# An order of steps written out for each engine, three idle PSUM banks taken into use, and two projections as 64-token column tiles

## The reference, cut to what matters

```python
# layer 0: non-local attention (32 inner channels)
th, ph, g = conv1x1(x, Wt, bt), conv1x1(x, Wp, bp), conv1x1(x, Wg, bg)
a = softmax(einsum('bci,bcj->bij', th, ph), -1)
x = conv1x1(einsum('bij,bcj->bci', a, g), Wo, bo) + x
t = to_tokens(x)                      # (4, 256, 64)
# layer 1: causal attention, 4 heads of 16, then a mixture of 8 experts
t = t + attn(layernorm(t), W_attn, W_proj)
t = t + experts(layernorm(t))         # gate weights from a mean over the batches
x = from_tokens(t)
```

## Time and profile before

| | us |
|---|---|
| median of 3 runs (lowest, highest) | 77.64 (77.51, 77.99) |
| time of the profiled execution | 77.84 |
| its span, first to last instruction | 76.0 |
| outside the span | 1.84 |
| PE busy | 66.5 (87%) |
| DVE busy | 47.9 (63%) |
| ACT busy | 36.1 (47%) |
| POOL busy | 15.9 (21%) |

### The profile page before, as it was taken

One profiled execution on the slowest core, in us unless ns is written; L12 is line 12 of the kernel. 1 busy time (PEld: TensorE's weight loads), 2 busy tenths in 40 slices (PEclk: granted clock), 3 DMA queues, 4 the chain that ended last, 5 costly groups with the idle time before them and its releaser, 6 DMA issues.

```text
span 76.0 us, 1446 instructions
## 1 busy us (share of the span) xinstructions
PE 66.5 (87%) x535; PEld 43.6 (57%) x535; DVE 47.9 (63%) x145; ACT 36.1 (47%) x74; POOL 15.9 (21%) x27
## 2 busy tenths in 40 slices
PE   3999984958896989999999999799959999999960
PEld 1328963946774774676667765457246274556520
DVE  2020668988589799089759955980551964799460
ACT  0604543072375067407640954249754458697500
POOL 3000033333320591041033203260312300000000
PEclk9999999999999999999999999999999999999999
DMA  0895000000000000000000000000000000000003
GB/s 5 238 301 237 0 0 0 0 0 0 9 0 4 0 0 0 0 9 0 0 0 0 0 0 9 0 0 4 0 0 0 0 0 9 0 0 0 0 34 103
DMA packets 961, 1.83 MB, mean 24 GB/s; under 512 B 120, under 2 KB 569, under 8 KB 955
## 3 DMA queue, kind: packets, MB, share of 16 engines
q1 hardware_dynamic: 732, 1.54, 6.2%
q10 hardware_dynamic: 222, 0.21, 1.1%
HBM read 1.48 MB, written 0.26 MB: 23 GB/s over the span
## 4 chain that ended last, share of the span: by engine, by line
PE 64%; DVE 13%; issue 8%; ACT 8%; POOL 3%; POOLq 0%; ACTq 0%
PE A L667 27%; PE M L667 15%; PE Q L667 10%; PE PR L667 8%; ACT p L456 4%; DVE m L599 3%; DVE m L595 3%; PE Q L687 2%; DVE m L565 2%; DVE th_s L495 2%; DVE ph_s L495 2%; POOL diag L307 1%; ACT h L412 1%; POOL ln_rs L362 1%; POOL xsum L392 1%
## 5 line engine op out<-in xcount | busy, mean ns | idle before, releaser
L307 POOL TENSOR_TENSOR diag<-neg_ident,m 128x256 fp32r<-128x256 f32 (+1 forms) x8 | 6.6, 826 | 21.6 <-DVE m L565 13.4
L362 POOL TENSOR_TENSOR ln_rs<-ln_var,half 128x2 f32<-128x2 f32 x8 | 5.6, 700 | 21.0 <-DVE ln_var L538 21.0
L412 ACT ACTIVATE h<-PR,bn_c,bn_s 128x256 f32<-128x256 f32 (+1 forms) x13 | 7.8, 637 | 2.1 <-PE PR L667 2.0
L402 ACT ACTIVATE qk_tmp<-PR 128x512 fp32r<-128x512 f32 x8 | 4.3, 594 | 7.5 <-PE PR L667 7.5
L456 ACT ACTIVATE p<-A 128x512 f32<-128x512 f32 (+1 forms) x8 | 6.0, 808 | 2.9 <-PE A L667 2.9
L552 DVE TENSOR_SCALAR ln_xs<-t,ln_mv,ln_rs 128x128 f32<-128x128 f32 x16 | 4.8, 343 | 3.3 <-POOL ln_rs L362 3.3
L667 PE MATMUL M<-warm 128*128 128x512 bf16 x10 | 4.4, 629 | 1.2 <-DVE warm L497 1.2
L667 PE MATMUL M<-p,v 128*32 128x256 f32 (+1 forms) x64 | 4.9, 333 | 0.4 <-ACT p L456 0.2
L599 DVE TENSOR_REDUCE m<-A 128x4 f32<-128x1024 f32 x4 | 4.9, 1214 | 0.0
L595 DVE TENSOR_REDUCE m<-A 128x4 f32<-128x512 f32 x4 | 2.8, 691 | 3.0 <-PE A L667 2.8
L402 ACT ACTIVATE f_tmp<-Q 128x512 fp32r<-128x512 f32 x4 | 2.4, 598 | 4.7 <-PE Q L667 4.7
(11 more groups left out here) (134 smaller groups left out, 138.8 us busy)
## 6 DMA issues: line engine op xcount, KB each, us to landing
pack_ffn<-in_pack_ffn_dram SPq DMA_DIRECT2D x1, 712.0 KB, 5.9
pack_attn<-in_pack_attn_dram SPq DMA_DIRECT2D x1, 276.0 KB, 3.9
out_dram<-o_sb SPq DMA_DIRECT2D x2, 128.0 KB, 1.7
x<-in_x_dram SPq DMA_DIRECT2D x1, 195.0 KB
pack_conv<-in_pack_conv_dram ACTq DMA_DIRECT2D x1, 130.5 KB
pack_ident<-in_pack_ident_dram ACTq DMA_DIRECT2D x1, 70.0 KB, 3.6
x<-in_x_dram SPq DMA_DIRECT2D x1, 65.0 KB
```

Of the source, the lines that this page charges most:

```text
L307: return engine.tensor_tensor(out, neg_ident[:, :].unsqueeze(1).to_broadcast([P, n, P]), m.unsqueeze(2).to_broadcast([P, n, P]), ALU.mult)
L362: pool.tensor_tensor(ln[i]["rs"][b][:, :], ln[i]["var"][b][:, :], half[:, 0:NB], ALU.pow).then_inc(ln[i]["s_pow"], 1)
L402: return act.activation(out, in_, ACT.Copy)
L412: act.activation(out, bank, ACT.Relu, bias=bn_c[:, i, q:q + 1], scale=bn_s[:, i, q:q + 1]).then_inc(relu_ok[s], 1)
```

## The change

The front no longer comes from the slot table. Each of PE, ACT, DVE and POOL gets a tuple `front` of (step, batch) pairs, and the slot table takes over from slot 7 (`FRONT_SLOTS`), which begins with the attention scores of batch 0. Three banks that stood idle at the time are used: the transposed scores go to A[2] for even batches and Q[0] for odd ones, and the weighted values of batches 0 and 2 go to PR[1] and Q[1], those of batch 1 to M. One filler matmul goes. DVE's layer-norm statistics become a step of their own (3.05); those of batch 3 and the normalization of batches 2 and 3 now stand in slot 7. Steps 5 and 9 split each half of 128 tokens in two column tiles of 64, so that eight instructions take the place of four. The residuals of batches 2 and 3 are issued in turn. The waits are those that the new banks need. The diff, cut to its core (only the import of itertools and unchanged lines are left out):

```diff
@@
         sums = [A[:, 2, 0:N], M[:, N:2 * N]]
-        pv1 = [bank[:, 0:NB * (C + 1)].rearrange("p (n c) -> p n c", n=NB) for bank in (A[:, 1, :], A[:, 0, :], A[:, 1, :], M)]
+        pv1 = [bank[:, 0:NB * (C + 1)].rearrange("p (n c) -> p n c", n=NB) for bank in (PR[1], M, Q[1], M)]
+        s1t = [(A[:, 2, :], Q[0])[b % 2] for b in range(B)]
         vps = Q[0][:, 0:NB * C]
@@
-        FILL = {"loads": 10, 1: 1, 2: 1}
-        CONV_STEPS = 4
+        FILL = {"loads": 10, 1: 1}
+        BATCH_OF = {2.8: 3, 3: 3, 3.05: 3, 3.1: 2, 3.15: 3}
         KEYS_ON_PE = 1
...
                       12.0: (0, 1, 0), 12.1: (0, 1, 1), 12.2: (0, 1, 2), 12.3: (0, 1, 3), 13.0: (1, 0, 0)}
+        FRONT_SLOTS = 7
         SLOTS = 1 + ATTN_SLOT[10] + 2 * (B - 1)
...
                 return FFN_SLOT[step] if b == 0 else None
-            if step in (0.9, 1):
-                return b + 1 if (b < 2) == (step == 1) else None
-            if step in (3.1, 3.2) and (b == B - 1) != (step == 3.2):
-                return None
-            if step == 3.2:
-                return ATTN_SLOT[6.2]
+            if step in BATCH_OF:
+                return FRONT_SLOTS if b == BATCH_OF[step] else None
             if step in (10, 10.2) and (b == 2) != (step == 10.2):
...
                 return None
-            if step < CONV_STEPS:
-                return int(step) + b
             return ATTN_SLOT[step] + 2 * b
...
         def schedule(*order):
-            for slot in range(SLOTS):
+            for slot in range(FRONT_SLOTS, SLOTS):
                 for step in order:
@@
-            for step, b in schedule(9, 6, 10, 10.2, 7, 0.9, 1, 3):
-                if step in (0.9, 1):
+            front = ((1, 0), (1, 1), (1, 2), (3, 0), (1, 3), (3, 1), (3, 2))
+            for step, b in itertools.chain(front, schedule(9, 6, 10, 10.2, 7, 3)):
+                if step == 1:
                     if b == 0:
@@
-            for step, b in schedule(8, 10.2, 11.3, 0, 0.1, 2, 5.1, 5.2, 10, 8.2, 5, 11.0, 11.1, 5.6, 7, 11.2, 12.0, 12.2, 4):
+            front = ((0, 0), (0.1, 0), (0, 1), (0.1, 1), (0, 2), (0.1, 2), (2, 0), (0, 3), (0.1, 3), (2, 1), (2, 2), (4, 0),
+                     (2, 3), (5.1, 0), (5.2, 0), (4, 1), (5.6, 0), (5, 0))
+            for step, b in itertools.chain(front, schedule(8, 10.2, 11.3, 5.1, 5.2, 10, 8.2, 5, 11.0, 11.1, 7, 11.2, 12.0, 12.2, 4)):
                 if step == 0:
@@
                     act.wait_ge(s1t_ps, b + 1)
-                    act.activation(p1[b][:, :, :], Q[(b + 1) % 2][:, :].rearrange("p (n i) -> p n i", n=NB),
+                    act.activation(p1[b][:, :, :], s1t[b].rearrange("p (n i) -> p n i", n=NB),
                                    ACT.Exp).then_inc(p1_ok, 1)
@@
-            for step, b in schedule(6, 8.1, 6.1, 6.2, 3.2, 0.9, 1, 3, 0, 5.1, 5.3, 3.1, 9, 12.1, 9.1, 12.3, 8, 7, 2):
+            front = ((0, 0), (1, 0), (0, 1), (0, 2), (1, 1), (1, 2), (2, 0), (0, 3), (3, 0), (3.05, 0), (1, 3), (3.1, 0),
+                     (3, 1), (3.05, 1), (3, 2), (3.1, 1), (5.1, 0), (3, 3), (3.05, 2))
+            for step, b in itertools.chain(front, schedule(6, 8.1, 6.1, 6.2, 3.1, 5.1, 5.3, 3.05, 3.15, 9, 12.1, 9.1, 12.3, 8,
+                                                           7)):
                 if step == 0:
...
                                 Q[b % 2][:, i * N:(i + 1) * N]).then_inc(f_split, 1)
-                if step in (0.9, 1):
+                if step == 1:
                     v.wait_ge(s1_ps, b + 1)
@@
                     i.then_inc(t1_ok, 1)
+                if step == 3.05:
                     layer_norm(0, b, t1[b], t1_ok)
-                if step in (3.1, 3.2):
+                if step in (3.1, 3.15):
                     normed(0, b, t1[b])
@@
-            def residual(b):
-
-                pe.wait_ge(t2_ok, b + 1)
+            def residual(*batches):
+
+                pe.wait_ge(t2_ok, batches[-1] + 1)
                 for n in range(NB):
-                    side = (b % SB) * C
-                    mm(sums[b // SB][side:side + C, n * P:(n + 1) * P], t2[b][:, n, :], ident, start=(n == 0),
-                       stop=False)
+                    for b in batches:
+                        side = (b % SB) * C
+                        mm(sums[b // SB][side:side + C, n * P:(n + 1) * P], t2[b][:, n, :], ident, start=(n == 0),
+                           stop=False)
@@
-            for step, b in schedule(8, 10.2, 6, 8.1, 8.15, 0.9, 3, 0, 0.1, 1, 2, 2.1, 5.1, 5, 10, 8.2, 8.25, 11.0, 7, 7.1, 5.5, 9,
-                                    11.2, 12.0, 12.2, 9.9, 4):
+            front = ((0, 0), (0.1, 0), (0, 1), (0.1, 1), (1, 0), (0, 2), (0.1, 2), (2, 0), (1, 1), (2.1, 0), (1, 2), (0, 3),
+                     (0.1, 3), (2, 1), (3, 0), (1, 3), (2.1, 1), (2, 2), (2.1, 2), (3, 1), (2, 3), (3, 2), (4, 0), (2.1, 3),
+                     (5.1, 0), (3, 3), (5, 0), (4, 1), (5.5, 0))
+            for step, b in itertools.chain(front, schedule(8, 10.2, 6, 8.1, 8.15, 5.1, 5, 10, 8.2, 8.25, 11.0, 7, 7.1, 9, 11.2,
+                                                           12.0, 12.2, 9.9, 4)):
                 if step == 0:
@@
                         pe.wait_ge(f_split, 2 * (b - 1))
-                    if b > 2:
-                        pe.wait_ge(p1_ok, b - 2)
                     for i in range(2):
@@
                     last.then_inc(vx_ps, 1)
-                if step in (0.9, 1):
+                if step == 1:
...
                         pe.wait_ge(m1_ok, b - 1)
-                    if b > 2:
-                        pe.wait_ge(t1_ok, b - 2)
                     if b == 0:
@@
-                    pe.wait_ge(f_split, 2 * min(b + 2, B))
-                    if b == 0:
-                        keep_busy(2, Q[(b + 1) % 2][:, :])
+                    pe.wait_ge(f_split, 2 * (3 if b == 1 else b + 1))
                     if b > 1:
...
                     for n in range(NB):
-                        mm(Q[(b + 1) % 2][:, n * N:(n + 1) * N], ph_s[b][:, n * P:(n + 1) * P], th_s[b][:, :],
+                        mm(s1t[b][:, n * N:(n + 1) * N], ph_s[b][:, n * P:(n + 1) * P], th_s[b][:, :],
                            start=(n == 0), stop=False)
...
                     for n in range(NB):
-                        last = mm(Q[(b + 1) % 2][:, n * N:(n + 1) * N], ones_r[:, :],
+                        last = mm(s1t[b][:, n * N:(n + 1) * N], ones_r[:, :],
                                   diag1[b][:, :, :].rearrange("p n i -> p (n i)"), start=False, stop=(n == NB - 1))
...
-                    pe.wait_ge(m1_ok, min(b + 2, B))
+                    if b == 2:
+                        pe.wait_ge(f_split, 2 * B)
+                    if b == 3:
+                        pe.wait_ge(t1_ok, 2)
                     pe.wait_ge(p1_ok, b + 1)
@@
                     else:
-                        pe.wait_ge(p1_ok, B - 1)
+                        pe.wait_ge(t1_ok, B - 1)
                         pe.wait_ge(ln[0]["s_TT"], b)
...
-                    pe.wait_ge(p1_ok, B)
+                    if b == 0:
+                        pe.wait_ge(p1_ok, B)
+                    else:
+                        pe.wait_ge(v_ok, b)
                     if b > 2:
...
                     for n in range(NB):
-                        last = mm(vps[:, n * C:(n + 1) * C], xT[b][0:C, n * P:(n + 1) * P], attn_v)
+                        for t in range(2):
+                            last = mm(vps[t * C:(t + 1) * C, n * C:(n + 1) * C],
+                                      xT[b][0:C, n * P + t * C:n * P + (t + 1) * C], attn_v)
                     last.then_inc(v_ps, 1)
@@
                         pe.wait_ge(v_const, 5)
-                        pe.wait_ge(t1_ok, B - 1)
+                        pe.wait_ge(m1_ok, B)
+                        pe.wait_ge(p1_ok, B - 1)
                     pe.wait_ge(q_ok, b + 1)
@@
                     for n in range(NB):
-                        last = mm(Q[0][:, n * C:(n + 1) * C], yT[b][:, n * P:(n + 1) * P], attn_proj)
+                        for t in range(2):
+                            last = mm(Q[0][t * C:(t + 1) * C, n * C:(n + 1) * C],
+                                      yT[b][:, n * P + t * C:n * P + (t + 1) * C], attn_proj)
                     last.then_inc(pj_ps, 1)
@@
             pe.wait_ge(cw_ok, 1)
-            for b in range(SB, B):
-                residual(b)
+            residual(SB, SB + 1)
             second_layer(2, 2)
...
             third_layer(0, 3)
```

More of the change, by code:

```diff
@@ L1 @@
 from contextlib import ExitStack
+import itertools
 import numpy as np
```

## The result

The changed kernel takes 75.46 us (median of six executions), the one before 77.58 (also of six) in the same series. The ratio is 0.969, 95% interval 0.964 to 0.974, which is 2.4 us (2.0 to 2.8). Some executions of nearly every version, the one before too, are 1.5 to 12% longer; they are in these two medians but not in the ratios, and nothing is read from a stretch that such an execution lengthened.

A forecast was written before the change was run, and what follows sets the result against it. Bounds: engine hand-offs in the front up to 25.41 us, then attention turns as a loop, with PE nearly continuous behind. 77.84 - 1.5 (front) - 0.5 (tiles) = 75.8, median 0.20 lower: 75.6 us, range 74.7 to 76.6.

The forecast's parts named there:

- The front: Everything before the first attention maximum at 25.41 us; the new order brings it 1.5 us earlier, bounds 1.1 to 1.8.
- The walk: Front events timed in the new order from the old trace's durations and distances; queries' copy at 20.15 against 21.67.
- the bounds given for the hand-offs: In the front, hand-offs of 0.13 to 0.15 us shrink where PE loaded weights ahead, four times, +0.3.
- 0.4 to spare: Normalization of batch 0 on DVE ends at 17.7, 0.4 us before PE's transposes of batch 0 at 18.07.
- They hide under ACT's copies: Transposes of batch 1, at about 21.0 on PE, hide under ACT's copies of queries and keys.
- each 0.1 us goes straight onto the keys: If batch 1's transposes are late in the front, each 0.1 us of it delays the keys.
- The moved layer norm: Layer-norm work moved into DVE's first attention turn leaves 0.2 us spare; cost nothing, bound +0.6.
- Column tiles: 64-token tiles gain 0.24 us each in the projections of batches 2 and 3, 0.5 in all; bounds -1.1 and 0.6.
- The residuals in turn: Alternating residuals of batches 2 and 3, followed by a block waiting for an ACT ReLU: 0, bound 0.1 either way.
- The rule against these tiles: Same-row tiles' weight loads would not overlap matmuls; eight loads alone 0.43 us, gain mostly gone; the trace was held to disagree.
- The clock: Rival: without the filler, PE's granted clock falls in the front, three us lost, 78.6; chance 0.04.
- The sum: Whole kernel: 1.5 us from the front and 0.5 from column tiles, 77.84 to 75.8, median 75.6.

The follow-up runs named there:

- the norm-first order: The changed kernel with DVE doing batch 0's output and layer-norm statistics before splitting batch 3, PE and ACT reordered too; ratio 0.971 to the kernel before.
- The six copies: The changed kernel with six more unused 128 x 128 copies on DVE in the first attention turn; ratio 0.974 to the kernel before.
- the order-alone run: The changed kernel with the blocks of steps 5 and 9 back at 128 tokens, without column tiles; ratio 0.983 to the kernel before.

## Why the prediction was right

- **The front, 1.5 us forecast, 1.71 measured.** The walk named the right events in the right order, and they came at most 0.35 us earlier than walked. On the old axis (0.12 subtracted) scores of batch 2 came at 11.73 (forecast 11.72), theta and phi of batch 3 at 12.04 (12.12), batch 3's scores at 14.75 (14.94), the normalization's end at 17.71 (17.7), the copy of the queries at 19.96 (20.15). What was mis-sized is small: from theta and phi to their copy 1.06 in place of 1.17 where PE had its weights ahead, and from the exponential to the values 0.05 (15.62 + 0.60 to 16.27) in place of 0.13. Both were within the bounds given for the hand-offs.
- **"0.4 to spare" was wrong, without a price.** The normalization of batch 0 ended at 16.94 + 0.89 = 17.83, and with the hand-off of 0.13 the transposes could start at 17.96, which they did (17.97). That its end met the forecast's 17.7 is luck: on the old axis it began at 16.82, some 0.3 earlier than walked, and took 0.89 for the 0.60 of the sum (the last section has the reason). PE, 0.2 earlier than walked, was ready for the transposes at about the same time. DVE's chain and PE's were equally long here, so neither alone could have been shortened with profit; the norm-first order shortened both.
- **"They hide under ACT's copies" was wrong, by 0.14 us.** The transposes of batch 1 are copied ahead of the keys on ACT, and with 128-token values they come too late. The forecast had named the price ("each 0.1 us goes straight onto the keys") but set the overrun to nothing; the tiles of batch 0's values, which I had costed at nothing, took it away again. From the queries' copy to the maximum it was 23.82 - 20.08 = 3.74, as forecast, by these two errors together; without the tiles it was 3.88 (23.96 - 20.08, where the copy of the queries is at 20.08 as well).
- **The moved layer norm cost nothing,** as forecast: 0.29 us of DVE's idle time are left for the 0.2 of the sum, and the turn is 7.24. The six copies put the reserve at 0.37.
- **Column tiles, 0.5 us from two projections, measured 0.54, but as 0.20 and 0.34 and not as twice 0.24.** The tiled block of batch 2 takes 51.37 - 51.00 = 0.37 to its successor, not the 0.31 that I took from the weighted values' pace. For batch 3 I had only looked at the projection itself. From its start to the second expert block behind it were 59.65 - 58.19 = 1.46, now 57.44 - 56.38 = 1.06, so 0.40 are gone there (0.34 reach the end), more than the 0.24 of the sum and more than the 0.55 - 0.37 = 0.18 of a tiled block by itself; the timeline lists the first matmuls of the expert block between it and the projection's last ones. Why these two run into each other now was not tested. The sum was met in part by luck: one size too large, the other too small. The other six were worth nothing, but for the values of batch 0 above. The turns were not shortened by the tiled values or by the projections of batches 0 and 1. The residuals in turn, set to 0 with a bound of 0.1, gave 0.05, and with them the 0.60 behind the first maximum is complete (0.54 + 0.05 + 0.01 in the first turn).
- **The rule against these tiles** (the Trainium skill, "TensorE: Matmul & The Clock Gate", Part 3, "What overlaps and what doesn't": a weight load overlaps running matmuls only if the row group differs) does not hold here. Eight loads and eight matmuls of one row group took 0.37 us to the successor; by the estimate in the prediction from that page the loads alone would take 0.43.
- **The clock** did not fall in the front without the filler: in the changed kernel's page all slices are full. In the order-alone run it fell only in the last half microsecond of the span (0.64), about 2 us after PE's last matmul.
- **The sum** was 2.0 us for 2.31 in the trace (1.71 + 0.60) and 2.4 (2.0 to 2.8) in time. The mechanism was right in both parts; what it fell short by is the hand-offs in the front (0.2) and the crumbs behind it (0.1).

## What to carry to other kernels

A wait on a buffer and a place in an in-order queue hide each other: free banks alone gave 0.00 us, the new order on the old banks 0.61, both together 1.71. Judge such changes together, by a walk over one iteration with durations and start-to-start distances from the trace; it met the events named above within 0.2 us, the exponentials and values in between within 0.35. And a faster block is worth something only where the trace shows no other engine ending the next wait: of eight tiled blocks, five gave nothing, and the other three 0.14, 0.20 and 0.34.

## What was not expected of the hardware

- The first matmul on x starts between 5.18 and 5.97 us after the span's start in profiles of these kernels, with the same instructions ahead of it. That alone is 1% of the time, as much as the smaller effects here, and counting from this matmul brought repeated events to 0.01 us (17.87 and 17.86).
- DVE took longer beside POOL, which the walk had left out. In the new order the diagonal of batch 3 runs on POOL while DVE normalizes batch 0. The timeline of the changed kernel, POOL and DVE:

```profile
12.38 1.36 POOL L305 TENSOR_TENSOR diag<-neg_ident,m 128x256 fp32r<-128x256 f32 x2 [1.57 <-DVE m L569]
...
13.17 0.59 DVE L515 TENSOR_TENSOR bn_d<-pack_attn 128x8 f32<-128x8 f32 x1
...
16.87 0.61 POOL L305 TENSOR_TENSOR diag<-neg_ident,m 128x256 fp32r<-128x256 f32 x1
```

  One of the two normalizations took 0.63 us for its usual 0.34, so that the pair started at 16.94 took 0.89 and not 0.60; POOL's operation ended at 17.48 in the midst of it. A subtraction of 128 x 8 numbers (bn_d) took 0.59 and ended at 13.76, when POOL's second diagonal ended (12.38 + 1.36 = 13.74). In the kernel before it had taken 0.16 with POOL idle:

```profile
12.87 0.16 DVE L514 TENSOR_TENSOR bn_d<-pack_attn 128x8 f32<-128x8 f32 x1
```

  The 0.3 us that the normalization lost were its spare time before the transposes, so they cost next to nothing here. In the norm-first order the pair took 0.60 again, with POOL's diagonal 0.8 us behind it, while bn_d, still beside a diagonal, took 0.59. No run took POOL's work away to prove it; the ends that coincide and this pair are the evidence. The Trainium skill states such a lock ("SBUF — State Buffer", under "SBUF: two separate sides": a port pair that DVE and GpSimd share is held for a whole instruction, and the other one blocks), and the trace agrees with it for these two operations.
